# A selective state-space stage on one core: the product with a chunk's finished sum one step later on VectorE, and the next chunk's first sum behind TensorE's other matmuls of its step

## What is computed

```python
delta = jax.nn.softplus(jnp.einsum('blr,dr->bld', delta_raw, W_dt) + b_dt)
A = -jnp.exp(A_log)
def step(h, inp):
    d_t, u_t, B_t, C_t = inp
    dA = jnp.exp(d_t[:, :, None] * A[None])
    h = dA * h + (d_t * u_t)[:, :, None] * B_t[:, None, :]
    y_t = jnp.einsum('bdn,bn->bd', h, C_t)
    return (h, y_t)
...
y = ys.transpose(1, 0, 2) + D_param * u
y = y * jax.nn.silu(z)
return jnp.einsum('bld,ed->ble', y, W_out)
```

## Time and profile before

| | |
|---|---|
| median of three runs | 3414.61 us (3413.39 to 3415.78) |
| the profiled execution | 3417.45 us, of which the span from first to last instruction is 3415.5 |
| busy: TensorE, VectorE, ScalarE, GpSimd | 3183.4 (93%), 2447.2 (72%), 1778.2 (52%), 1578.5 us (46%) |
| first scans of batches 1, 2, 3 | 231.4, 381.6, 531.9 us, so 150.25 us a batch |
| last instruction of VectorE in the stage | 1271.7 us |

### The profile page before, as it was taken

The page is one execution under the profiler, slowest core; times in us unless marked ns, Lnnn a source line. Parts: engine busy times, 40 slices in busy tenths (PEclk is TensorE's granted clock), DMA queues, the critical chain, the costliest instruction groups (busy, mean ns, idle before and its releaser), DMA issues. The chain is left out here.

```text
span 3415.5 us, 50699 instructions
## 1 busy us (share of the span) xinstructions
PE 3183.4 (93%) x16204; PEld 1869.8 (55%) x16204; DVE 2447.2 (72%) x3702; ACT 1778.2 (52%) x4150; POOL 1578.5 (46%) x970
## 2 busy tenths in 40 slices
PE   5999999999999876999999799999999999999997
PEld 2354545455454444666666456666666666666665
DVE  6999999999999984767777556655555556555553
ACT  4768686777768543655556333333333433333332
POOL 1766667666666640000000355445554455555552
PEclk9999999999999998999999899999999999999999
DMA  4767677676767744000100000000001100000000
GB/s 123 252 213 252 213 245 235 213 265 216 253 215 245 246 155 127 25 25 25 36 25 19 19 1 19 18 18 18 18 18 37 51 24 25 25 25 25 25 12 19
DMA packets 146654, 343.29 MB, mean 101 GB/s; under 512 B 14898, under 2 KB 78470, under 8 KB 146582
## 3 DMA queue, kind: packets, MB, share of 16 engines
q1 hardware_dynamic: 138134, 334.02, 29.1%
q10 hardware_dynamic: 8448, 8.39, 0.7%
HBM read 320.87 MB, written 21.50 MB: 100 GB/s over the span
## 5 line engine op out<-in xcount | busy, mean ns | idle before, releaser
L535 POOL TENSOR_TENSOR hb<-bcB,du 128x1024 f32<-128x1024 f32 x256 | 602.2, 2353 | 378.3 <-DVE hb L668 345.2
L657 DVE TENSOR_TENSOR_SCAN ps_dA<-ps_dA,hb 128x1024 f32<-128x1024 f32 x256 | 585.7, 2288 | 54.8 <-ACT ps_dA L860 54.8
L1112 PE MATMUL ps_y<-hb,ident 128*128 128x512 f32 x1024 | 484.8, 602 | 33.0 <-DVE hb L668 32.9
L1947 POOL TENSOR_TENSOR c_pr<-c_pr,c_inv 128x512 f32<-128x512 f32 (+1 forms) x256 | 233.8, 935 | 381.3 <-DVE c_inv L2069 381.3
L1477 ACT ACTIVATE b_pr<-b_ps_s,b_negmax 128x256 f32<-128x256 f32 (+1 forms) x512 | 263.8, 527 | 166.2 <-DVE b_negmax L1391 164.8
L2186 ACT ACTIVATE c_pr<-c_ps_s,c_negmax 128x256 f32<-128x256 f32 (+1 forms) x512 | 223.7, 447 | 226.5 <-DVE c_negmax L2051 149.6
L1112 PEld LDWEIGHTS ps_y<-hb,ident 128*128 128x128 f32 x1024 | 189.2, 192 | 258.3 <-issue 187.9
L860 ACT ACTIVATE ps_dA<-delta,a_neg 128x511 f32<-128x511 f32 x512 | 330.0, 676 | 1.1
L668 DVE TENSOR_TENSOR hb<-ps_dA,bcC 128x1024 f32<-128x1024 f32 x256 | 311.9, 1218 | 5.9
L2430 PE MATMUL c_ps_s<-c_hT,c_w 128*128 128x512 f32 x576 | 261.3, 599 | 0.9 <-ACT c_hT L2229 0.9
L1924 POOL TENSOR_TENSOR c_q_cos<-c_q_cos,c_q_sin 128x1024 f32<-128x1024 f32 x64 | 150.9, 2357 | 231.6 <-DVE c_q_sin L2031 231.6
(11 more groups left out here) (241 smaller groups left out, 6179.8 us busy)
## 6 DMA issues: line engine op xcount, KB each, us to landing
bcB<-bc_scratch SPq DMA_DIRECT2D x256, 512.0 KB, 4.7
bcC<-bc_scratch SPq DMA_DIRECT2D x256, 512.0 KB, 4.7
c_x<-stream_scratch SPq DMA_DIRECT2D x16, 512.0 KB, 5.2
c_xr<-stream_scratch SPq DMA_DIRECT2D x16, 512.0 KB, 4.1
xn<-in_x_dram SPq DMA_DIRECT2D x8, 512.0 KB, 4.9
xr<-in_x_dram SPq DMA_DIRECT2D x8, 512.0 KB, 7.7
x_scratch<-xr SPq DMA_DIRECT2D x8, 512.0 KB, 6.9
b_x<-x_scratch SPq DMA_DIRECT2D x8, 512.0 KB, 4.4
```

Source lines behind the costliest of these rows:

```text
L535: pool.tensor_tensor(hb[:, s % RING, :, :], bcB[:, s % ROWS, :, :], bc(du[:, c % 2, :].unsqueeze(1), [P, NG, T]), ALU.mult)\
L657: dve.tensor_tensor_scan(flat(h_all), flat(h_all), flat(tile), 0.0, ALU.mult, ALU.add)\
L1112: last = pe.matmul(ps_y[:, :], W["ident"][:, :], hb[:, r % RING, i, :], start=False, stop=(g == GROUPS - 1 and i == NG - 1))
L1947: pool.tensor_tensor(rows, rows, bc(inv[:, u, :].unsqueeze(2), [P, 2, w]), ALU.mult)\
```

## The change

On VectorE, `gate_y` for chunks 0 to 2 moves from behind the scan of steps 8, 16 and 24 to behind the scan of steps 9, 17 and 25. (The last chunk's product stays where it is, behind the scan of the next batch's step 0.) On TensorE, in steps 9, 17 and 25 the product with u and the chunk's first unit of sums are issued behind the step's other matmuls instead of ahead of them. No instruction is added or left out.

```diff
                     dve.tensor_tensor_scan(flat(h_all), flat(h_all), flat(tile), 0.0, ALU.mult, ALU.add)\
                         .then_inc(scanned.s, 1)
-                    if g == 0 and c:
+                    if g == 1 and c:
                         gate_y(b, c - 1)
                     if s == 0 and prev:
                         gate_y(b - 1, IC - 1)
...
             def body(b, prev, more):
 
+                def sum_unit(r):
+                    c, g = unit(r)
+                    if g == 0:
+
+                        pe.wait_ge(y_ready.s, y_ready.at(b, c))
+                        pe.matmul(ps_y[:, :], diag_d[:, c, :], u[:, c, :], start=True, stop=False)\
+                            .then_inc(y0_done.s, 1)
+                    pe.wait_ge(weighed.s, weighed.at(b, r + 1))
+                    for i in range(NG):
+                        last = pe.matmul(ps_y[:, :], W["ident"][:, :], hb[:, r % RING, i, :],
+                                         start=False, stop=(g == GROUPS - 1 and i == NG - 1))
+                    last.then_inc(summed.s, 1)
+
                 for s in range(SCANS + 1):
-                    if s >= 1:
-                        r = s - 1
-                        c, g = unit(r)
-                        if g == 0:
-
-                            pe.wait_ge(y_ready.s, y_ready.at(b, c))
-                            pe.matmul(ps_y[:, :], diag_d[:, c, :], u[:, c, :], start=True, stop=False)\
-                                .then_inc(y0_done.s, 1)
-                        pe.wait_ge(weighed.s, weighed.at(b, r + 1))
-                        for i in range(NG):
-                            last = pe.matmul(ps_y[:, :], W["ident"][:, :], hb[:, r % RING, i, :],
-                                             start=False, stop=(g == GROUPS - 1 and i == NG - 1))
-                        last.then_inc(summed.s, 1)
+
+                    late = s in (GROUPS + 1, 2 * GROUPS + 1, 3 * GROUPS + 1)
+                    if s >= 1 and not late:
+                        sum_unit(s - 1)
                     if s < SCANS:
...
                         if more:
                             prepare(b + 1, s, prev)
                         ffn(b, s, prev, more)
+                    if late:
+                        sum_unit(s - 1)
```

## The result

The change made the kernel slower: 3428.07 us (median of six runs, 3425.72 to 3430.82) against 3415.20 us for the kernel before on the same chip (3413.39 to 3418.49). The ratio is 1.0036, with an interval of 1.0026 to 1.0047: +12.9 us, about +9 to +16. I had forecast +22.4 us, 3437 us in a range of 3421 to 3453. So direction and range hold, and the forecast change is 1.7 times the measured one. The profiled execution after took 3428.56 us with a span of 3426.6, which is 11.1 us more than the span before; the mean granted clock of TensorE is 0.976.

A forecast was written before the change was run, and what follows sets the result against it. TensorE was taken to bound steps 0 to 23, VectorE and ScalarE steps 24 to 28. Terms of 16.7 us (batches 1 to 6), 3.1 (batch 0) and 2.6 (batch 7) made 3414.6 + 22.4 = 3437 us, range 3421 to 3453.

The forecast's parts named there:

- What bounds the batch: TensorE sets steps 0 to 23, so VectorE's leads from steps 8 and 16 are worth 0.
- Rival 3: VectorE's waits in steps 8 to 22 are real and at most 22.0 us come back: 3393 us, chance 0.05.
- Step 25, +2.58 us: Matmuls moved between the up projection and the transposes of h count in full: +2.58 us a batch.
- Rival 4: The late unit at step 25 is hidden, something else holding the transposes: 3415 to 3419 us, chance 0.04.
- Step 17, +0.55 us: TensorE reaches L953 before the next batch's last u is there and waits: +0.55 us a batch.
- Step 24, -0.35 us: VectorE's 0.26 us wait and about 0.1 us of handover go from the chain to the Silu: -0.35 us.
- I keep this loss as it is: The 1.75 us that the low clock costs at step 25's up projection and the unit behind stays unchanged.
- my own sign (2.6 us in most batches): If step 25's up projection takes 2.6 us or over 5 us in most batches, the clock moved the time.
- rival 2: Idle times fall so the clock does not drop in the up projection: 14 us less, 3423 us, chance 0.13.

The follow-up runs named there:

- e2: The change at steps 9 and 17 only, against the kernel before, step 25 keeping its old order: 3416.25 us, ratio 0.9999.
- e3: The change at step 25 only, against the kernel before: 3427.08 us, ratio 1.0030.
- e12: The kernel before with three added matmuls on zeros behind the up projection of step 25: 3434.30 us, ratio 1.0052.
- e5: The changed kernel with step 25's late product with u and first unit of sums put ahead of the up projection: 3407.75 us, 0.9981 of the kernel before.
- e1: VectorE's half of the change alone, TensorE's order as in the kernel before: 3424.13 us, ratio 1.0023.
- e7: The kernel before with three added matmuls on zeros in TensorE's wait ahead of step 25's up projection: 3409.01 us, ratio 0.9981.
- e9: The changed kernel with both units of sums of step 25 ahead of its up projection: 3410.30 us, 0.9979 of the kernel before.
- e6: The kernel before with its unit of sums between step 25's up projection and the transposes moved ahead of that projection: 3411.23 us, ratio 0.9988.
- e8: The changed kernel with two added matmuls on zeros in TensorE's wait ahead of step 25's up projection: 3426.25 us, 1.0032 of the kernel before.

## Why the prediction was right, and where its size was off

**What bounds the batch: right.** TensorE sets steps 0 to 23, and VectorE's leads there are worth nothing. The trace after has `h` of step 22 at the same 97.28, and e2 shows it with 0.9999. Rival 3 (the waits are real) is out. Of what VectorE doesn't wait for at steps 8 and 16 (2.88 us in batch 2), 0.82 us is a wait for the decay at step 9 and 1.90 us are added ahead of steps 20 to 22, as forecast. In batch 0 alone `h` comes 0.37 us later (95.40 instead of 95.03).

**Step 25, +2.58 us: right.** In the batches in which the up projection is no faster than before, the scan of step 29 is 2.35 us later, 2.58 less the 0.24 of step 24. e3 has the whole cost, e12 has it without the move (+2.59), and e5 takes it away. Rival 4 (hidden) is out.

**Step 17, +0.55 us: wrong, its lower end was right.** L953 starts 76.74 us after the first scan (461.65 less 384.91). Before, the product with u started in this place, at 76.65 (458.29 less 381.64). The new wait is at most 0.09 us. I had set the table load of L756 behind the last convolution. ScalarE in batch 2, after, and under it TensorE's last convolution:

```profile
459.62 1.28 ACT L756 ACT_TABLE_LOAD   x1
460.91 0.69 ACT L756 ACTIVATE u<-ps_p,cols 128x512 f32<-128x512 f32 x1
...
456.41 3.60 PE L948 MATMUL ps_p<-xin,diag_c 128*128 128x512 f32 x8
```

The convolution ends at 460.01, and the load began at 459.62, ahead of that. So here it did not wait for the convolution, and started as soon as ScalarE was free of the decay (458.30 and 1.30 us for the pair). It is so in each of batches 1 to 6, by 0.38 to 0.40 us. The last u is there at 461.60, just 0.05 us ahead of L953. The term was 0.55 in six batches and 0.5 in batch 0, 3.8 us of the sum.

**Step 24, -0.35 us: right, a little large.** 0.24 is measured, from the start of the up projection, in batches 1 to 6. In batch 0, for which I had no gain, it starts 0.50 us later (121.61 instead of 121.11).

**The clock: the step that failed.** I wrote "I keep this loss as it is", and put all of the chance of another outcome into rivals that would have it so in every batch. In fact it changed in some, in four of the first seven: by my own sign (2.6 us in most batches) the clock moved the time. With 2.6 us of idle time ahead of z's projection instead of 0.86, the clock falls there already in six of batches 0 to 6 (3.12 to 3.65 us for what took 1.98; in batch 4 it doesn't). That costs nothing: TensorE waits for the Silu all the same, 2.56 us instead of 4.26, and the up projection starts at the same time. In batches 0, 2, 3 and 5 the up projection then runs at 2.63 us, where it took 5.06, 4.07, 4.13 and 4.25 before. So rival 2 came true in half of the batches. In units of the sum: eight times 2.34 are 18.7 us. Back come 2.1 us in batch 0 (net of its later start), 1.7 in each of batches 2, 3 and 5, and 0.7 in batch 7, together 7.9, which leaves 10.8.

So of the 22.4 us, 3.8 were a wait that isn't there, and the other 18.6 came as 18.7, of which 7.9 were paid back by a faster up projection. The result lies in the range because the largest term was right, and because the range had room for all of rival 2. My own range of 3430 to 3444 was also added up wrongly at its upper end: step 17 at 1.8 us and step 24 at 0 make 3448.

That the low clock moved, from the up projection to z's projection where it costs nothing, is likely but not shown. For it: in the changed kernel and e3, batches 0 to 6, the up projection is at full clock in eight of the twelve batches in which z's projection is slow, and in neither of the two in which z's projection takes 1.98 us (batch 4 after, batch 5 of e3). Against it as the only way: in batches 2 and 5 of e1 and in 1 and 3 of e12 the up projection is at full clock, behind 2.89 and 3.70 us of idle time, with z's and the gate projection at full clock too.

The Trainium skill (TensorE: Matmul & The Clock Gate, "What's actually happening") says that activity releases the throttle. What I drew from it, that more idle time brings more of the low clock, held for z's projection (3.12 to 3.65 us instead of 1.98) and not for the up projection behind it. Why the clock falls in one batch and not in the next at the same idle time, the runs don't settle. e12 shows that the length of the wait ahead doesn't decide it: 3.70 us in both, and 4.33 us in one and 2.63 in the other.

## What to carry to other kernels

- Before a wait is worth removing, look for the engine that has no idle time in that stretch. Here VectorE gave up 2.88 us of waits a batch for nothing, because TensorE was the one that was busy for 106.00 of 106 us.
- A group of matmuls in an engine's idle time, ahead of a wait, is free, and the same group behind the wait costs its whole length: 2.59 us a batch in e12, where the clock is the same. Work that must come later goes into the next idle time, ahead of its wait (e5, 3407.75 us, faster than the kernel before and the changed one).
- A gain is sure only at the end of the batch. e7 was 1.69 us early at step 29 and kept 0.74. e9 took more off the path than e5 and was no faster (0.9979 against 0.9981), because a longer wait came up at the batch's end with the low clock behind it.

## What the runs showed of the hardware

- **The low clock after a wait comes in some batches and not in others.** The same eight matmuls behind the same 3.70 us took 4.33 or 2.63 us in one execution (e12), and one unit of sums behind the same 2.56 us took 3.61 or 1.98 us (e6, ahead of batches 5 and 4). Filling 2.75 us of the wait kept the clock up in batches 0 to 6 of e7, but filling part of a longer one not in two of the batches of e8.
- **A small instruction of VectorE can take as long as POOL's beside it.** L125 went from 0.19 to 1.14 us and L130 from 1.15 to 2.68, each beside a product of POOL that had started first. The Trainium skill (SBUF — State Buffer, "Who interferes with whom") has this as a lock on a pair of ports that the two engines share, held for a whole instruction by the one that comes first. The traces agree: L125 ends 0.04 us behind POOL's product, and L130 0.74 us behind its (521.89). L130 of e7, which starts 0.40 us before a product of POOL ends (L535, 517.99 to 520.34), still takes 1.15 us.
- **A table load of ScalarE can start before the input of its activation is complete.** It ran from 459.62, and the activation's input was finished at 460.01, by the end of the matmul as the profile models it. In step 16 of the same batch, though, the load for chunk 2's u (454.95) stood idle until 0.10 us behind its convolution's end, which I can't explain.
